# Graph attention layer: W1 and its products ahead of the first transposes, and GpSimd normalises one tile of four

## The reference

```python
h = jnp.maximum(_layernorm(x, axis=-1), 0.0)        # x: (4096, 256)
# graph attention on h, adj: (4096, 4096) of 0 and 1
h = inp @ W1 + b1
e = jax.nn.leaky_relu((h @ a1)[:, None] + (h @ a2)[None, :] + b2, ALPHA)   # ALPHA = 0.2
attention = jnp.where(adj > 0, e, jnp.float32(-1000000000000.0))
attention = jax.nn.softmax(attention, axis=1)
h_prime = attention @ h
return jax.nn.elu(h_prime)
# result: x + that
```

## Time and profile before

| | us |
|---|---|
| median of 3 runs | 423.12 |
| lowest and highest | 422.97, 427.16 |
| the profiled execution | 423.61 |
| its span | 421.82 |
| TensorE busy | 416.8 (99%) |
| VectorE busy | 373.9 (89%) |
| ScalarE busy | 308.7 (73%) |
| GpSimd busy | 30.4 (7%) |

### The profile page before, as it was taken

How to read it: one execution, slowest core, us unless ns; L and a number is a source line. 1 busy time by engine, 2 the same in 40 slices (tenths; PEclk the granted TensorE clock), 3 DMA queues, 4 the chain that set the end, 5 groups by cost and what they waited for, 6 DMA issues and landing times.

```text
span 421.8 us, 8476 instructions
## 1 busy us (share of the span) xinstructions
PE 416.8 (99%) x3347; PEld 411.0 (97%) x3347; DVE 373.9 (89%) x404; ACT 308.7 (73%) x306; POOL 30.4 (7%) x44
## 2 busy tenths in 40 slices
PE   9999999999999999999999999999999999999996
PEld 8888899999999999999999999999999999999996
DVE  4897999999998499999995799999992999999945
ACT  4789898999983769957564888768574789586622
POOL 1021100000000400000000400000001200000243
PEclk9999999999999999999999999999999999999999
DMA  8950068555557346648388066647477166576302
GB/s 273 392 209 0 2 215 336 200 200 199 199 200 263 137 170 231 207 147 295 114 309 292 32 211 238 247 144 263 138 266 284 68 232 207 193 246 237 115 4 97
DMA packets 22585, 82.40 MB, mean 195 GB/s; under 512 B 1531, under 2 KB 14113, under 8 KB 14242
## 3 DMA queue, kind: packets, MB, share of 16 engines
q1 hardware_dynamic: 22276, 81.81, 54.9%
q10 hardware_dynamic: 286, 0.27, 0.2%
HBM read 77.86 MB, written 4.21 MB: 195 GB/s over the span
## 4 chain that ended last, share of the span: by engine, by line
PE 97%; DVE 2%; ACT 0%; issue 0%; POOL 0%; DVEq 0%; ACTq 0%; POOLq 0%
PE ps L773 53%; PE ps L775 27%; PE ps L653 5%; PE ps L795 2%; PE ps L796 2%; PE ps L797 2%; PE ps L596 2%; PE ps L641 2%; DVE adj_s L881 1%; DVE h_raw L866 0%; DVE y L1088 0%; PE ps L749 0%; PE ps L730 0%; PE ps L622 0%; PE ps L672 0%
## 5 line engine op out<-in xcount | busy, mean ns | idle before, releaser
L775 PE MATMUL ps<-hp_lo,w_hi 128*128 (+1 forms) x936 | 226.8, 282 | 0.0
L773 PE MATMUL ps<-hp_hi,w_hi 128*128 (+1 forms) x936 | 226.7, 282 | 0.0
L881 DVE SCALAR_TENSOR_TENSOR adj_s<-R,p,adj_s 128x1024 f32<-128x1024 f32 x128 | 165.1, 1330 | 24.2 <-ACT adj_s L451 24.0
L773 PEld LDWEIGHTS ps<-hp_hi,w_hi 128*128 128x128 f32 x936 | 176.8, 189 | 0.0
L775 PEld LDWEIGHTS ps<-hp_lo,w_hi 128*128 128x128 f32 x936 | 176.7, 189 | 0.0
L459 ACT ACTIVATE w_hi<-adj_s 128x2048 fp32r<-128x2048 f32 x64 | 122.3, 1911 | 40.0 <-DVE adj_s L881 39.7
L891 DVE SCALAR_TENSOR_TENSOR w_lo<-adj_s,w_hi 128x2048 fp32r<-128x2048 f32 x64 | 146.0, 2282 | 0.0
L451 ACT ACTIVATE adj_s<-adj_s 128x2048 f32<-128x2048 int32 x64 | 122.2, 1909 | 22.9 <-DMA adj_s<-adj_t 22.5
L773 PE MATMUL ps<-hp_hi,w_lo 128*128 (+1 forms) x944 | 123.1, 283 | 0.0
L773 PEld LDWEIGHTS ps<-hp_hi,w_lo 128*128 128x128 f32 x944 | 117.3, 189 | 0.0
L358 POOL TENSOR_TENSOR y<-y,h_sum 128x2064 f32<-128x2064 f32 x3 | 12.8, 4260 | 271.0 <-ACT y L534 271.0
(11 more groups left out here) (110 smaller groups left out, 193.7 us busy)
## 6 DMA issues: line engine op xcount, KB each, us to landing
adj_s<-adj_t SPq DMA_DIRECT2D x64, 1024.0 KB, 4.9
x_s<-x SPq DMA_DIRECT2D x7, 512.0 KB, 9.0
o_s<-x SPq DMA_DIRECT2D x3, 1024.0 KB, 7.7
out<-o_s SPq DMA_DIRECT2D x6, 512.0 KB, 6.8
R<-r_rows SPq DMA_DIRECT2D x1, 1536.0 KB, 6.4
adj_s<-x SPq DMA_DIRECT2D x1, 1024.0 KB, 5.6
out<-adj_s SPq DMA_DIRECT2D x8, 128.0 KB, 1.7
x_s<-x SPq DMA_DIRECT2D x2, 256.0 KB, 3.9
```

The lines of the kernel that those rows point to most:

```text
L773: last = pe.matmul(acc, block_w, hh, start=fresh, stop=False)
L775: pe.matmul(acc, block_w, hl, start=False, stop=False)
L881: last = dve.scalar_tensor_tensor(sgn, R[:, ds(ic * CW, CW)], p[:, ds(source(r, c) + s, 1)], sgn, ALU.max, ALU.mult)
```

## The change

`WARM` goes from 11, 2, 5, 2 to 9, 1, 3, 5 multiplications. TensorE turns W1 before the vectors, and weighs W1 before b1 and before the transposes of group 0. ScalarE's list is put in another order to match: W1 transposed is kept first, the root of group 0 stands before `repeat_b1`, and the products are kept before the first ReLU. GpSimd normalises the last tile of each group, as x times the inverse plus the shift; VectorE keeps one tile of groups 0 to 3 and none of groups 4 to 7; ScalarE's share stays. GpSimd's tiles of groups 4 to 7 stand between its exponents. TensorE waits for one more semaphore before each group's transposes.

```diff
-WARM = (11, 2, 5, 2)
+NORM_POOL = 1
+NORM_DVE = 4
+WARM = (9, 1, 3, 5)
...
+            def normalise(g):
+
+                pool.wait_ge(rstd_ready, g + 1)
+                if g >= XN:
+                    pool.wait_ge(tp_ready, KC * (g - XN + 1))
+                for t in range(GT - NORM_POOL, GT):
+                    tile = g * GT + t
+                    last = pool.tensor_scalar(xn[:, g % XN, t, :], x_s[:, tile, :], rstd[:, tile:tile + 1],
+                                              shift[:, tile:tile + 1], ALU.mult, ALU.add)
+                last.then_inc(xn_pool, 1)
+
+            for g in range(4):
+                normalise(g)
             pool.wait_ge(g3_ready, 1)
-            for g in range(GROUPS - 1):
+            for g in range(4):
+                exponents(g)
+                normalise(g + 4)
+            for g in range(4, GROUPS - 1):
                 exponents(g)
...
             act.wait_ge(pool_c, 1)
+            keep_WT()
             keep_acol()
-            repeat_b1()
             act.wait_ge(eps_ready, 1)
             root(0)
+            repeat_b1()
+            normalise(0)
             keep_b1()
-            normalise(0)
-            keep_WT()
+            keep_wv()
             keep_ba()
             relu_T(0)
-            keep_wv()
             root(1)
...
                 pe.wait_ge(xn_act, g + 1)
-                pe.wait_ge(xn_dve, g + 1)
+                if g < NORM_DVE:
+                    pe.wait_ge(xn_dve, g + 1)
+                pe.wait_ge(xn_pool, g + 1)
...
             pe.wait_ge(pool_c, 3)
+            turn_W1()
             turn_vectors()
             spread_b1()
-            turn_W1()
             keep_warm(WARM[1])
+            weigh()
             weigh_b1()
             keep_warm(WARM[2])
             transposes(0)
-            weigh()
             keep_warm(WARM[3])
...
-                for t in range(NORM_ACT[g], GT):
+                for t in range(NORM_ACT[g], GT - NORM_POOL):
...
-            normalise(4)
...
-            normalise(5)
...
-            normalise(6)
...
-            normalise(7)
```

More of the change, by code:

```diff
@@ L195, in build @@
         xn_dve = sem("xn_dve")
+        xn_pool = sem("xn_pool")
         tp_ready = sem("tp_ready")
```

## The result

The changed kernel takes 427.02 us (median of 21 runs, 425.36 to 428.78) against 423.15 us (422.65 to 427.16) before: it is slower by 0.7%, ratio 1.0073 with a 95% interval of 1.0058 to 1.0089. The 3.9 us between the medians are a little more than the ratio says, because the new times lie in three groups: nine runs at 425.4 to 425.8 us, with a granted clock of 0.994 to 0.995 over the whole span, ten at 427.0 to 427.2 (0.991 to 0.992, one of them 0.998) and two at 428.8 (1.00). The profiled execution is of the first group: 425.69 us with a span of 423.4 us; so the profile shows the lowest group, and not the median. The median was forecast at 423.3 us with a range up to 424.4 us.

A forecast was written before the change was run, and what follows sets the result against it. The prediction took the opening to be paced by when TensorE may start its transposes and projections. Group 1's later start gave +0.18 us (step 3's 0.10 contained in it), other terms 0: median 423.3 us, range 422.4 to 424.4 us.

The forecast's parts named there:

- Steps 1 and 2: TensorE's opening and ScalarE's queue: W1's transposes fill warming places, cost 0; root 0.13 to 0.2 us earlier, repeated b1 0.3 later.
- Step 3: TensorE up to the first projection: idle for 0.5 us, group 0's transposes +0.28 us, first projection +0.10 us.
- rival (b): TensorE's clock in the opening: late W1 or 0.5 us idle brings second 1.2 GHz stretch, 2.6 us, 425.7 us; chance 0.05.
- Step 4: Group 1, ScalarE's root and tiles: group 1's transposes start 0.14 to 0.21 us later, and the span gets this.
- rival (d): GpSimd's first tile alone costs 6.4 us, so group 0's transposes start 4.4 us later; 427.5 us; chance 0.02.
- Step 5: GpSimd's tile: 0.73 us, upper end 0.9, starting when VectorE's tile has ended; cost to group 1 taken as 0.
- (c): GpSimd's tile costs 6.4 us by itself and every group's transposes wait for it; +23 us, 446 us; chance 0.02.
- Step 6: VectorE is rid of eight tiles, some 3 us, none of it on the path; gain 0.
- Step 7: GpSimd's queue, exponents now behind tiles: cost 0, at worst a turn late by a few tenths.
- the sum: Whole kernel: +0.18 us on the span, taking the median to 423.3 us.

## Why the prediction was wrong

- **Steps 1 and 2** held. W1's transposes filled the places of warming records, b1 repeated ended at 7.32 us (7.40 forecast), the root stood at 6.72 (6.8).
- **Step 3 failed, and with it the dismissal of rival (b)**. The wait before the weighing was 0.56 us (0.5 forecast), but I priced it as idle time and nothing more, and priced the products behind it by the spacings of before, which are those of 2.4 GHz. Group 0's transposes came at 10.38 instead of 9.81 us and took 1.72 instead of 0.9; the projection came at 13.37 instead of 11.85 us. Those 1.52 us are what the lowest of the three groups lost there; the upper ones lose some 1.4 and 3 us more. The run with the wait filled has no slow record behind the rise and gives 424.1 us.
- **Step 4** held as a chain, and its cost came from step 3 alone: the root of group 1 stood at 13.13 us (11.57 before), ScalarE's tiles ended at 14.95 (13.39) and the loads of group 1's transposes began at 15.02 (13.46), each 1.56 us later where 0.14 to 0.21 were forecast. The bias addition forecast for 40.75 us came at 42.19.
- **Rival (b) named this** and had 0.05. I dismissed it by the earlier trace rows, where the weight loads rest for 1.2 of 5 us at a clock of 1.00. That stretch is full of products that move 128 to 258 columns; a share of loads at rest says nothing of how much the products move. The right question was what else stands between the clock's rise and the first transposes: the change had put eight more narrow records and an idle stretch there, and had left two of fourteen warming records. The 425.7 us of rival (b) agree with the lowest group by luck: the span grew by 1.6 us and not by 2.6, since the second slow stretch was shorter than the first, and 0.5 us lie around the span; the median is 1.3 us higher. The 427.5 us of rival (d) are near the median by luck too.
- What was wrong in rival (b) too: it asked for a wait. The run without one still took 425.4 us, and with the products widened seven of ten runs were at 424.0 or less. Idle time (the run with a stretch put into the kernel before, and four warming records fewer ahead of it) does it as well. So narrow products and idle time each have a part, by one pair of kernels each; how they weigh against each other in the changed kernel itself stays open, after four runs of the kernel that was to tell. That the new order and warm-up bring the clock down, and that filling the wait undoes it, is shown.
- **Step 5** held: 0.56 to 0.65 us against 0.73 (the two tiles that started under a tile of VectorE's took 0.64 and 0.65, the other six 0.56), and the 6.40 us of the earlier trace rows was waiting for the most part. In the run with the tile alone the same subtraction started 0.1 us ahead of VectorE's second mask (398.35 us), which reads two tiles, and took 0.92 us; in the changed kernel it started in the middle of that mask (399.96 to 401.24) and took 5.88, ending 0.7 us behind VectorE's two-input work:

```profile
397.15 2.61 DVE L902 SCALAR_TENSOR_TENSOR adj_s<-R,p,adj_s 128x1024 f32<-128x1024 f32 x2
398.24 0.92 POOL L385 TENSOR_SCALAR adj_s<-adj_s 128x256 f32<-128x256 f32 x1 [68.65 <-DMA adj_s<-x]
```
```profile
398.76 2.47 DVE L902 SCALAR_TENSOR_TENSOR adj_s<-R,p,adj_s 128x1024 f32<-128x1024 f32 x2
400.49 5.88 POOL L385 TENSOR_SCALAR adj_s<-adj_s 128x256 f32<-128x256 f32 x1 [69.28 <-DMA adj_s<-x]
401.16 4.48 DVE L912 SCALAR_TENSOR_TENSOR w_lo<-adj_s,w_hi 128x2048 fp32r<-128x2048 f32 x2
```

  So rivals (c) and (d) are out: no tile took several microseconds, the first (0.64 us) included. By the Trainium skill's page SBUF — State Buffer, section Who interferes with whom, a VectorE instruction with two inputs in SBUF contends with a GpSimd instruction that reads SBUF, and whichever issues first has the shared pair of ports. The trace agrees for GpSimd, which waited out VectorE's work in the changed kernel; VectorE's mask behind the 0.92 us tile was held much less, 1.42 us instead of 1.28.
- **Step 6** held: VectorE's 3 us bought nothing, since the bias addition still waited 0.43 us for TensorE ahead of 42.19 us.
- **Step 7** held: the turn that needs the exponents found them done at 25.58, ahead of 26.94 us.
- **What the sum left out**: 0.47 us around the span, with GpSimd's eight tiles.

## What to carry to other kernels

That TensorE is listed as busy did not keep its clock up here; when a change takes warming products out, or puts narrow products (a few columns) or a wait in their place, price the stretch behind it at half speed as well. A narrow product that is paced by its weight load can be widened almost for nothing (the kernel before with it: ratio 1.0009). Where runs fall into groups some microseconds apart, look at the pace of equal records in the opening before looking for a contended resource.

## What the hardware showed that I had not expected

- A TensorE that was listed as busy throughout lost its clock (the profile of the kernel without the wait; seven of its ten runs have the same clock, 0.994 to 0.996) while fourteen of its records moved 2 columns or one. With twelve of them at 128 columns it held the clock through a wait of 0.47 us, and in the changed kernel so widened through 0.86 us, in one profile each.
- The column of the granted clock shows 1.00 for the microseconds before its first record. At 9.5 to 12 us it shows 1.00 for 12 records in one kernel and for 22 in another; the pace is the surer sign.
- The clock of the same kernel goes several ways in the opening: it rises in time or late, and falls back for a shorter or a longer stretch. The 21 times of the changed kernel differ by 3.4 us, in three groups; the mean clock is 0.994 to 0.995 in the first, 0.991 to 0.992 in nine of ten of the second and 1.00 in the third.
- A GpSimd tensor_scalar of 128 x 256 takes 0.56 us undisturbed, and adds about 0.06 us around the span.
